# A state-space layer and a ternary feed-forward on eight cores: the first two blocks are computed during the weight preparation

## What is computed

```python
def _quant_weight(w):                     # ternary weights
    s = clip(mean(abs(w)), EPS, None)
    return clip(round(w / s), -1, 1) * s
def _quant_act(x):                        # 8 bit rows
    scale = 127 / clip(max(abs(x), axis=-1, keepdims=True), EPS, None)
    return clip(round(x * scale), -128, 127) / scale
def _bitlinear(x, w): return einsum('bsi,oi->bso', _quant_act(x), _quant_weight(w))

# x: (4, 8192, 1024) f32; W_in (64, 1024), W_out (1024, 64), w1 (4096, 1024), w2 (1024, 4096)
def attn(x):                              # a diagonal state-space layer with 64 states
    u = einsum('bld,nd->bln', x, W_in)
    h = scan over l: h * Abar + u_l * Bbar ; y_l = h * C
    return einsum('bln,dn->bld', y, W_out)
def ffn(x): return _bitlinear(gelu(_bitlinear(x, w1)), w2)

x = x + attn(layernorm(x))
x = x + ffn(layernorm(x))
```

## Time and profile before

| | us |
|---|---|
| median of 3 runs (lowest to highest) | 1217.36 (1216.73 to 1220.47) |
| profiled run, its own time | 1216.07 |
| profiled run, span of its slowest core (others from 1210.3) | 1214.5 |
| TensorE busy, share of the span | 993.4, 82% |
| VectorE | 740.9, 61% |
| ScalarE | 361.6, 30% |
| GpSimd | 113.1, 9% |
| start of the first mm1, of mm1(2) | 269.0, 329.1 |

### The profile page before, as it was taken

The page is one execution under the profiler, slowest core; times in us unless marked ns, Lnnn a source line. Parts: engine busy times, 40 slices in busy tenths (PEclk is TensorE's granted clock), DMA queues, the critical chain, the costliest instruction groups (busy, mean ns, idle before and its releaser), DMA issues.

```text
span 1214.5 us, 14169 instructions; the slowest of 8 cores (1210.3 to 1214.5 us)
## 1 busy us (share of the span) xinstructions
PE 993.4 (82%) x4612; PEld 442.1 (36%) x4612; DVE 740.9 (61%) x1166; ACT 361.6 (30%) x455; POOL 113.1 (9%) x231
## 2 busy tenths in 40 slices
PE   3880000025999999999999999999999999999997
PEld 1330000012444444444444444444444444444443
DVE  5760653845666666666666666666666666665661
ACT  3117788712222222222222222222222222222110
POOL 1220000010000110000011000000110001000000
PEclk9995555558999999999999999999999999999999
DMA  8799492042444433433343444443444443343322
GB/s 263 230 287 342 154 339 74 7 97 49 78 99 98 94 87 89 95 87 87 87 88 87 98 94 95 88 87 89 96 98 96 99 97 87 87 94 63 61 62 70
DMA packets 214169, 136.00 MB, mean 112 GB/s; under 512 B 201424, under 2 KB 201552, under 8 KB 210000
## 3 DMA queue, kind: packets, MB, share of 16 engines
q1 hardware_dynamic: 204880, 101.53, 36.2%
q0 software_dynamic: 9216, 33.56, 8.5%
HBM read 67.96 MB, written 16.78 MB: 70 GB/s over the span
## 4 chain that ended last, share of the span: by engine, by line
PE 80%; DVE 7%; DMA 5%; ACT 4%; issue 2%; DVEq 1%; SPq 0%; ACTq 0%; another core or an unknown queue 0%; POOLq 0%; POOL 0%
PE pout L527 37%; PE pm L500 37%; DVE T L380 6%; DMA W<-w1t 4%; ACT sgn L262 2%; PE py L481 2%; PE pu L509 2%; PE py L482 2%; PE py L517 1%; DMA W<-W 1%; ACT sgn L251 1%; PE py L518 1%; DMA W<-xo 0%; ACT sgn L257 0%; ACT pch L247 0%
## 5 line engine op out<-in xcount | busy, mean ns | idle before, releaser
L500 PE MATMUL pm<-T,W 128*128 128x512 fp8e4 x2048 | 451.6, 381 | 23.5 <-DMA W<-W 23.1
L527 PE MATMUL pout<-T,W 128*128 128x512 fp8e4 x2048 | 447.6, 379 | 1.5 <-DVE W L453 1.5
L435 DVE TENSOR_REDUCE sm<-W 128x1 f32<-128x1024 f32 x128 | 156.1, 1220 | 264.4 <-ACT W L276 264.4
L500 PEld LDWEIGHTS pm<-T,W 128*128 128x128 bf16 x2048 | 200.7, 98 | 269.9 <-issue 32.9
L527 PEld LDWEIGHTS pout<-T,W 128*128 128x128 bf16 x2048 | 197.8, 98 | 249.1 <-issue 14.7
L276 ACT ACTIVATE W<-pm,sm 128x512 f32<-128x512 f32 x256 | 171.6, 684 | 356.2 <-PE pm L500 355.3
L299 ACT CAST hb_s<-h_s 64x128 bf16<-64x128 f32 x32 | 9.5, 298 | 289.8 <-DVEq L406 289.8
L488 PE MATMUL pm<-sm,ones 128*128 128x1 f32 x4 | 1.1, 348 | 105.5 <-DVEq L371 105.5
L445 DVE TENSOR_SCALAR W<-W,sm 128x4096 f16<-128x4096 f32 x32 | 75.3, 2353 | 2.8 <-issue 0.4
L380 DVE SCALAR_TENSOR_TENSOR T<-W,sm,sgn 128x2048 fp8e4<-128x2048 f32 x32 | 73.0, 2349 | 4.7 <-ACT sgn L257 2.4
L509 PE MATMUL pu<-W,winTb 128*64 128x128 bf16 x256 | 21.1, 228 | 55.0 <-DMA W<-W 54.3
(11 more groups left out here) (103 smaller groups left out, 616.2 us busy)
## 6 DMA issues: line engine op xcount, KB each, us to landing
T<-xh SPq DMA_DIRECT2D x16, 1024.0 KB, 6.1
W<-w1t SPq DMA_DIRECT2D x8, 2048.0 KB, 32.8
W<-w2t SPq DMA_DIRECT2D x8, 2048.0 KB, 16.0
W<-xo POOLq DMA_DIRECT2D x32, 512.0 KB, 3.9
out<-W POOLq DMA_DIRECT2D x32, 512.0 KB, 6.6
W<-W SPq DMA_TRANSPOSE x96, 3.1
W<-winT SPq DMA_DIRECT2D x1, 256.0 KB, 4.5
T<-win SPq DMA_DIRECT2D x1, 256.0 KB, 6.1
```

The lines of the kernel that those rows point to most:

```text
L435: v.tensor_reduce(am4[:, j:j + 1], h[c % 2][:, j * 1024:(j + 1) * 1024], AX.X, ALU.max, apply_absolute_value=True)
L500: m = t.matmul(pm1[G % 3], k1T[c % 2][:, k, :], t1T[:, gi, k, :], start=(k == 0), stop=(k == 7))
L527: i = t.matmul(pout[:, d * 512:(d + 1) * 512], k2T[c % 2][:, m, :], t2T[:, m, d * 512:(d + 1) * 512], start=(m == 0), stop=(m == 31))
```

## The change

One SBUF area `BIG` of 200 KB per partition takes the place of W, T and sgn, and buffers share it by time. In preparation:

- xh comes in single chunks of 512 KB into 16 slots, and pG counts chunks. The pass starts ahead of the small coefficient computations, and the decay columns are made one by one in the pass.
- w1 is issued by GpSimd: tiles 0 to 5 after the statistics of chunks 18, 20, ... 28, tiles 6 and 7 behind the pass, as slots in them come free. GpSimd issues w2 too. xo chunks 0 and 1 are loaded by SyncE behind xh.
- Block 0 and block 1 up to k1 stand ahead of most of the |w1| sums. mm1(0) goes group by group behind w1's ternary passes, with its gelus between the compare passes; mm1(1), block 2 up to k1 and mm2(0) go into the w2 passes. Some |w| sums go to VectorE.
- Sign is written in fp8 into the place where the ternary value will stand, and each is followed by a drain.

In the steady loop, which now starts at b = 2, GpSimd's load is load(b+3), behind the store and ahead of inv1(b+3); k2h and k2b share one buffer, and drains stand behind k1b and k2b.

```diff
-RING = 6
+RING = 16
...
+    wtile = [at(16 * i, 4096) for i in range(NWT)]
+    t1g = [at(128 + 4 * g, 4096, FP8) for g in range(8)]
+    t1T = [t.rearrange("p (k j) -> p k j", k=8) for t in t1g]
+
+    t2g = [at(196, 4096, FP8)] + [at(4 * i, 4096, FP8) for i in range(7)]
+    t2T = [t.rearrange("p (m d) -> p m d", m=4) for t in t2g]
+    junk = t2g[0]
+
+    xr = [at(96 + 4 * j, D) for j in range(8)] + [at(160 + 4 * j, D) for j in range(8)]
...
+    h = [at(160, H), at(80, H)]
...
+            for c in range(NCH):
+                if c >= RING:
+                    sp.wait_ge(S["pG"], c - RING + 1)
+                sp.dma_start(out=xr[c % RING], in_=dr["xh"][c]).then_inc(S[f"xr{c % RING}"], 16)
+                if c == 7:
+                    sp.dma_start(out=winT_f, in_=dr["winT"][:, :]).then_inc(S["winl"], 16)
+                    sp.dma_start(out=win_f, in_=dr["win"][:, :]).then_inc(S["winl"], 16)
+                    sp.dma_start(out=wout_f, in_=dr["woutT"][:, :]).then_inc(S["wol"], 16)
+            for c in range(2):
+                sp.dma_start(out=xbe[c], in_=dr["xo"][c]).then_inc(S[f"xe{c}"], 16)
...
+            txn(0)
+            txn(1)
+            tk1(0)
+            tk1(1)
+            tk2(0)
+            txn(2)
+            tk1(2)
+            tk2(1)
+            txn(3)
+            txn(4)
+            for b in range(2, NCH):
+                if chunks(0, b + 3):
+                    txn(b + 3)
+                if chunks(0, b + 1):
+                    tk1(b + 1)
+                tk2(b)
...
+            def load_w1(i):
+                if i >= 6:
+                    g.wait_ge(S["pG"], 16 + 4 * (i - 5))
+                g.dma_start(out=wtile[i], in_=dr["w1t"][i]).then_inc(S[f"w{i}"], 16)
...
+                if c >= 18 and c % 2 == 0 and (c - 18) // 2 < 6:
+                    load_w1((c - 18) // 2)
+            load_w1(6)
+            load_w1(7)
...
             def load(c):
-                if c >= 3:
+                if c == 2:
+                    g.wait_ge(S["q2"], 2 * 2)
+                elif c < 5:
+                    g.wait_ge(S["q2"], 2 * 7)
+                else:
                     g.wait_ge(S["x2"], c - 2)
-                g.dma_start(out=xb[c % 3], in_=dr["xo"][c]).then_inc(S[f"xl{c % 3}"], 16)
-
-            g.wait_ge(S["q"], 4 * NWT)
-            for c in range(3):
-                load(c)
-            for b in range(-3, NCH + 2):
+                g.dma_start(out=xbs[(c - 2) % 3], in_=dr["xo"][c]).then_inc(S[f"xl{(c - 2) % 3}"], 16)
+
+            inv1(0)
+            inv1(1)
+            inv2_(0)
+            inv2_(1)
+            for i in range(NWT):
+                g.wait_ge(S["q1"], 2 * i + 2)
+                g.dma_start(out=wtile[i], in_=dr["w2t"][i]).then_inc(S[f"w{i}"], 16)
+            load(2)
+            inv1(2)
+            inv2_(2)
+            load(3)
+            load(4)
+            inv1(3)
+            inv1(4)
+            for b in range(2, NCH + 2):
                 c = b - 2
                 if chunks(0, c):
                     g.wait_ge(S["out"], c + 1)
                     g.dma_start(out=out_d[c], in_=x2[c % 4]).then_inc(S[f"od{c % 4}"], 16)
-                c = b + 3
-                if chunks(0, c):
-                    g.wait_ge(S["ve1"], c + 1)
-                    if c >= 2:
-                        g.wait_ge(S["xn"], c - 1)
-                    g.tensor_tensor(inv[c % 2], ve[c % 2], nhalf, ALU.pow)
-                    g.drain()
-                    g.tensor_tensor(nb1[c % 2], mv[c % 2][:, 0:1], inv[c % 2], ALU.mult)
-                    g.drain()
-                    g.tensor_scalar(nb1[c % 2], nb1[c % 2], -1.0, None, op0=ALU.mult)
-                    g.drain().then_inc(S["inv1"], 1)
-                c = b + 1
-                if chunks(0, c):
-                    g.wait_ge(S["ve2"], c + 1)
-                    if c >= 1:
-                        g.wait_ge(S["k1"], c)
-                    g.tensor_tensor(inv2, ve2, nhalf, ALU.pow).then_inc(S["inv2"], 1)
-                c = b + 4
-                if chunks(3, c):
-                    load(c)
+                if chunks(0, b + 3):
+                    load(b + 3)
+                    inv1(b + 3)
+                if chunks(0, b + 1):
+                    inv2_(b + 1)
...
+            def absum(w, part, acc, sem, lap):
+                s.wait_ge(S[f"w{w}"], 16 * lap)
+                s.activation(junk[:, 0:part], wtile[w][:, 0:part], AF.Abs, bias=0.0, scale=1.0,
+                             accum_out=acc[:, w:w + 1], saturate=False)
+                s.drain().then_inc(S[sem], 1)
...
+            for i in range(2):
+                absum(i, 4096, wab, "abs1", 1)
+            xnorm(0)
+            xnorm(1)
+            hbf(0)
+            hbf(1)
+            for i in range(2, 7):
+                absum(i, 4096, wab, "abs1", 1)
+            absum(7, 2048, wab, "abs1", 1)
+
+            s.wait_ge(S["thr1"], 1)
+            s.wait_ge(S["winT"], 1)
+            s.wait_ge(S["x2"], 2)
+            for g in range(8):
+                for j in (2 * g, 2 * g + 1):
+                    sign(j, t1g)
+                    s.drain().then_inc(S["sg1"], 1)
+                if g >= 2:
+                    gelu(0, g - 2)
+            gelu(0, 6)
+            gelu(0, 7)
+            for i in (0, 1, 3, 4, 6):
+                absum(i, 4096, wab2, "abs2", 2)
+            absum(7, 2048, wab2, "abs2", 2)
+            s.wait_ge(S["thr2"], 1)
+            for g in range(8):
+                if 1 <= g:
+                    s.wait_ge(S["q2"], 2 if g < 5 else 4)
+                for j in (2 * g, 2 * g + 1):
+                    sign(j, t2g)
+                    s.drain().then_inc(S["sg2"], 1)
+                if g < 2:
                     for gi in range(4):
-                        gelu(b, gi)
-                c = b + 3
-                if chunks(0, c):
-                    s.wait_ge(S["inv1"], c + 1)
-                    s.wait_ge(S[f"xl{c % 3}"], 16 * (c // 3 + 1))
-                    if c >= 2:
-                        s.wait_ge(S[f"xT{c % 2}"], 16 * (c // 2))
-                    s.activation(xn[c % 2], xb[c % 3], AF.Identity, bias=nb1[c % 2],
-                                 scale=inv[c % 2]).then_inc(S["xn"], 1)
-                if chunks(0, b):
-                    for gi in range(4, 8):
-                        gelu(b, gi)
-                c = b + 2
-                if chunks(0, c):
-                    s.wait_ge(S["scan"], c + 1)
-                    if c >= 2:
-                        s.wait_ge(S["y"], c - 1)
-                    s.copy(hb_s[c % 2], h_s[c % 2]).then_inc(S["hb"], 1)
+                        gelu(1, 4 * g + gi)
+                if g == 3:
+                    xnorm(2)
+                if g == 5:
+                    hbf(2)
+            xnorm(3)
+            hbf(3)
+            xnorm(4)
...
+            stats(0)
+            stats(1)
+            scan(0)
+            scan(1)
+            mix(0)
+            mix(1)
+            absum(7, 2048, 4096, wab[:, 8:9], 1)
+            v.wait_ge(S["abs1"], NWT)
+            threshold(1, wab, s1o)
+            for c in range(2):
+                v.tensor_scalar(a1[c], a1[c], s1o, None, op0=ALU.mult)
+            for j in range(16):
+                ternary(1, j, t1g)
+            for j in range(4):
+                hmax(0, j)
+            hquant(0)
+            absum(5, 0, 4096, wab2[:, 5:6], 2)
+            absum(7, 2048, 4096, wab2[:, 8:9], 2)
+            absum(2, 0, 4096, wab2[:, 2:3], 2)
+            v.wait_ge(S["abs2"], 6)
+            threshold(2, wab2, s2o)
+            v.tensor_scalar(a2[0], a2[0], s2o, None, op0=ALU.mult)
+            for j in range(6):
+                ternary(2, j, t2g)
+            for j in range(4):
+                hmax(1, j)
+            stats(2)
+            for j in range(6, 10):
+                ternary(2, j, t2g)
+            hquant(1)
+            v.tensor_scalar(a2[1], a2[1], s2o, None, op0=ALU.mult)
+            scan(2)
+            mix(2)
+            for j in range(10, 16):
+                ternary(2, j, t2g)
+            stats(3)
+            scan(3)
+            stats(4)
+            for b in range(2, NCH + 2):
...
+            mmu(0)
+            mmu(1)
+            mmy(0)
+            mmy(1)
+            total(1)
+            mm1(0)
+            total(2)
+            mm1(1)
+            mmu(2)
+            mmy(2)
+            mm2(0)
+            mmu(3)
+            for b in range(2, NCH + 1):
                 if chunks(0, b):
                     mm1(b)
                 if chunks(0, b + 2):
                     mmu(b + 2)
                 if chunks(0, b + 1):
                     mmy(b + 1)
-                if chunks(0, b - 1):
-                    mm2(b - 1)
+                mm2(b - 1)
```

409 lines of the change are left out of this document (223 added, 186 removed), and 4 rows, old and new, of the table SEMS.

## The result

| us | median (lowest to highest) | ratio to before, 95% interval |
|---|---|---|
| before | 1218.43 (1216.73 to 1220.47), 4 runs | |
| changed | 1370.95 (1369.52 to 1373.93), 4 runs | 1.1254 [1.1227, 1.1282] |

The change costs 12.5%. The forecast was 1282 with a range of 1225 to 1325: the sign is right, and the loss of 153 us is more than twice the 65 forecast. In some executions one die runs at a lower granted clock and takes longer, whatever the kernel; those are left out of every median here.

The account below looks back on a forecast made before the run. Preparation bounds the kernel to about 269 us, TensorE alone from mm1(2) at 329.28. Span 1214.5, less 38.7 for the head, plus 105 for the late x load, is 1281; with 1.6 around it 1282, range 1225 to 1325.

Parts of the forecast that it names:

- part 4: Steady loop: x load behind the store delays stats, xnorm and mm1 by 3.9 per block, +105 us over 27 blocks.
- C: Rival: TensorE's clock falls in each block's new idle stretch, costing 1.35 to 2.6 per block, 1318 to 1352; chance 0.12.
- A: The forecast itself, shorter head and late load in the steady loop: 1282 us; chance 0.56.
- mm1 is late by xnorm's start - 10.1: Steady block, in us from mm1's start: gelu 4 follows xnorm, and mm1's group 8, due at 12.1, needs gelu 4.
- Rival D: Steady loop: the load lands as if alone, 3.9 after issue, 0.3 lost per block, 1185 us; chance 0.14.
- the point where the sign turns: Steady loop: a block loses 1.43, with the load landing at 7.8, 5.0 after its issue.
- The head: All before mm1(2): mm1(2) starts at 290.6 instead of 329.28, a gain of 38.7 us.
- w1 was in: Preparation: the w1 loads finish at 107.5 instead of 123.9, at 341 GB/s without a pause.
- part 2: w1 compare passes and block 0, then the sums of w2: first w2 sign at 212 against 200.84.
- part 3: w2 passes and block 1: 78.6 us from the first w2 sign to mm1(2), which starts at 290.6.
- B: Rival, head: the drain doesn't hold inv1(0) for w1; first sign at about 112, 28 earlier, 1254 us; chance 0.10.
- E: Rival: Sign, Abs and Gelu don't share one table set, some 18 reloads of 1.28, 1305 us; chance 0.08.

Follow-up runs that it names:

- experiment 6: Changed kernel plus 12 useless TensorE matmuls before the wait of mm1's eighth group in 27 blocks; 1336.61 us, ratio 1.0979.
- experiment 1: Changed kernel with load(b+3) issued ahead of the wait for out(b-2) and its store; 1200.68 us, ratio 0.9857.
- experiment 2: Kernel before with only the load moved, from the end of a pass to behind the store; 1381.2 us, ratio 1.1337.
- experiment 4: Changed kernel with GpSimd's three drains in inv1 replaced by waits on a semaphore of its own; 1366.18 us, ratio 1.1214.
- Experiment 8: Kernel of experiment 5 with the head reordered: ScalarE's sums of w1 and VectorE's half sum moved ahead; 1182.37 us, ratio 0.971.
- experiment 5: Changed kernel with load(b+3) ahead of the store and its wait, and inv1's three GpSimd drains replaced by semaphore waits; 1189.50 us, ratio 0.9768.
- experiment 9: Kernel of experiment 5 with each w1 tile loaded in four DMAs of 4 KB rows instead of one of 16 KB rows; 1193.55 us.
- experiment 10: Kernel of experiment 8 with each w1 tile loaded in four DMAs of 4 KB rows instead of one of 16 KB rows; 1188.37 us.

## Why the prediction was right in sign and wrong in size

**The step that failed** is part 4's "3.9 per block". It measured 6.98, and the 27 passes make 83 us of the 89 between 1282 and 1371; the head makes the other 6. The step has two parts, which the table of experiment 6 separates.

- *The clock was put as a rival of A instead of a term of its sum.* C was given 0.12, because "the stretch here, 3.9, is hardly longer than the 3.4 after which the clock fell there". But the forecast's own path made that idle stretch, and there was a row for what such a stretch does. Given A, C was the likelier course, not a different one. It measured 1.97 per block, 53 us, inside C's own bounds of 1.35 to 2.6. Even so C's 1318 to 1352 misses the time, as it took over A's wait. The Trainium skill, "TensorE: Matmul & The Clock Gate", HAM oscillation, which the prediction quoted beside C, describes a loop of this kind; the rows at 632 to 639 and experiment 6 agree with it.
- *The wait was mis-sized.* From the start of the statistics, 0.1 behind the load's landing, to xnorm took 3.9 (15.13 less 11.24), forecast 3.7: right. But the statistics started 11.24 into mm1 in the mean (10.28 to 12.3), not 10.3. The store was issued at up to 2.85 instead of 2.2, and the load took 8.2 in the mean from issue to landing, where the forecast's 2.8 to 10.3 leaves 7.5. That makes 5.0 instead of 3.9, 30 us over 27 blocks, inside the bounds of 0.3 to 5.5.

The sum by these terms: 1214.5 - 32.3 + 27 x (5.0 + 1.97) = 1370.4.

**The path of part 4 was right** (late load, statistics, xnorm, gelu 4, eighth group), and experiments 1 and 2 show it from both sides: put in alone it costs 13.4%, taken out alone it brings the changed kernel below the one before. The relation "mm1 is late by xnorm's start - 10.1" held in every trace: 15.13 gives 5.0, 10.26 gives 0.13 to 0.16 for that block (14.11 instead of 13.98), 7.75 and 9.8 give nothing. Rival D (the load lands as if alone) had it at 1185; the point where the sign turns, 5.0 after issue, was passed by a median of 8.0.

**The head** came out 6.3 us later than forecast, and one term has that size. w1 was in at 113.9, not 107.5: 35.52 MB until 115 us moved at a mean of 309 GB/s (322 from 3.5 us to 113.9), and I had counted 341 from 3.5 us on, a rate of rows 2 that belongs to the last tiles only. The steps behind it held within 3 us, and that their two misses cancel is luck: xnorm(0) 115.45 (forecast 108.6), first Sign 147.18 (140.5), first Sign of w2 215.73 (212, so part 2 was 3 shorter than worked out), mm1(2) 296.85 (290.6, part 3 2.5 longer).

**The drain (B against A).** The drain in inv1(0) did wait for w1, and experiment 4 shows it by removing it. But B's price, 28 us, was wrong too: without the drain 5 us come back, because the transposes are slow beside w1's loads (10.6 and 7.5 us) and the sums, which B let follow the tiles, still stand behind the casts in ScalarE's stream. Experiment 8 brings 7 more by order alone.

**E** is refuted: one table load in the whole stretch, at 160.00.

## What to carry to other kernels

Before moving a transfer to "where its buffer is free anyway", look for the instruction that waits for it and count what stands behind that one in the same queue: here one 512 KB load, issued 11 us later in a pass of 29, outweighed a head shortened by 32 us, and moving two lines back made it a gain. If the forecast itself puts TensorE to wait a few microseconds in each pass of a loop, the fall of the clock belongs in the sum, not among the rivals. Keep a load ahead of the store that has to wait for a result; behind it, it inherits the wait and the store's time on the DMA engines. And where GpSimd's drains are taken out, put one back where nothing waits for GpSimd: the closing drain otherwise pays for all its DMAs.

## What the runs showed of the hardware

- A drain on GpSimd behind a DMA holds the next operation until that DMA has landed: 12.28 us for w1, 4.91 for a store, none when the drains are replaced (experiments 4 and 5).
- A drain on GpSimd also costs about 0.082 us for each DMA (of 128 rows, here) that GpSimd has issued since its last one, with all of them landed: 0.38 us behind 4, 5.29 behind 64, 6.43 behind 78, 8.4 behind 102. The kernels without any drain in the loop so end 8.5 to 11.6 us behind the last store instead of 3.6 to 3.9, and a single drain 87 us before the end restores that.
- Two queues share the DMA engines in turns that go by the row, not by the byte: beside 16 KB rows, x's 4 KB rows got 512 KB in 7.7 us, 68 of about 340 GB/s, the fifth that 4 to 16 gives; with equal rows they kept up with TensorE. In the changed kernel's trace until 115 us w1's queue has 1152 packets for 16.78 MB, 1024 of which would be one for each 16 KB row. The Trainium skill, "DMA: Bandwidth & Descriptors", Queues, rings and completion order, says that each engine goes round the queues packet by packet; that rows of four times the length take four times the share agrees with it.
- A transpose of 3.1 us alone takes far longer beside w1's loads: the second one of experiments 4, 5, 9 and 10 (7.5, 11.9, 28.3 and 21.5 us) landed within 2 us of w1's last tile, whatever the rows. Which share of the engines it gets there, no run here shows.
- Idle for 4.1 us, TensorE took up work at 633.87 and fell to half the clock (0.65 in the us from 634, 0.50 in the one from 636), until it was back at 2.4 GHz at 638. With 2.75 us of filler in that stretch it kept 2.4 GHz in 15 of 24 blocks.
